# Graph attention: the bound and the multiply of three of 25 source blocks move from VectorE to GpSimd

## The reference, cut to what matters

```python
h = (x @ W).reshape(n, HEADS, C)
a_s = jnp.einsum('nhc,hc->nh', h, att_src)
a_d = jnp.einsum('nhc,hc->nh', h, att_dst)
e = jax.nn.leaky_relu(a_s[src] + a_d[dst], 0.2)
m = jax.ops.segment_max(e, dst, num_segments=n)
p = jnp.exp(e - m[dst])
z = jax.ops.segment_sum(p, dst, num_segments=n)
alpha = p / (z[dst] + 1e-16)
out = jax.ops.segment_sum(h[src] * alpha[:, :, None], dst, num_segments=n)
```

## Time and profile before

| what | value |
|---|---|
| median of three runs | 2292.35 us (2290.55 to 2293.96) |
| the profiled execution, its own time | 2294.51 us |
| its span | 2292.8 us |
| busy: TensorE, VectorE, ScalarE, GpSimd | 81%, 77%, 52%, 5% |
| mean granted TensorE clock | 0.94 |
| HBM traffic | 149 GB/s over the span |

### The profile page before, as it was taken

One profiled execution on the slowest core, in us unless ns is written; L12 is line 12 of the kernel. 1 busy time (PEld: TensorE's weight loads), 2 busy tenths in 40 slices (PEclk: granted clock), 3 DMA queues, 4 the chain that ended last, 5 costly groups with the idle time before them and its releaser, 6 DMA issues. The chain is left out here.

```text
span 2292.8 us, 43438 instructions
## 1 busy us (share of the span) xinstructions
PE 1856.6 (81%) x16035; PEld 1418.4 (62%) x16036; DVE 1761.2 (77%) x1796; ACT 1188.8 (52%) x2187; POOL 122.4 (5%) x224
## 2 busy tenths in 40 slices
PE   3566666699778988889888898884999999798793
PEld 2466666344566766667666676673888887455452
DVE  4999998000589999999999999956888887671474
ACT  1466666000577777777777777655666665101001
POOL 4000000100000000000000000000000000110120
PEclk9899999799999999999999999967999999899896
DMA  3598999999043134441344413343555550790691
GB/s 110 152 251 250 250 251 250 240 272 272 15 117 103 39 94 116 117 106 35 93 116 117 108 35 91 90 105 68 115 125 127 120 115 1 328 408 18 270 417 56
DMA packets 482537, 341.78 MB, mean 149 GB/s; under 512 B 322664, under 2 KB 474496, under 8 KB 475824
## 3 DMA queue, kind: packets, MB, share of 16 engines
q1 hardware_dynamic: 478096, 337.57, 52.6%
q10 hardware_dynamic: 3664, 1.68, 0.3%
q0 software_dynamic: 720, 1.77, 0.3%
HBM read 214.05 MB, written 126.94 MB: 149 GB/s over the span
## 5 line engine op out<-in xcount | busy, mean ns | idle before, releaser
L1195 ACT ACTIVATE exponentials<-gr_ps,att_cols 128x256 f32<-128x256 f32 (+1 forms) x1300 | 487.6, 486 | 183.2 <-PE gr_ps L1050 180.6
L1050 PE MATMUL gr_ps<-ident,gr_r 128*128 128x128 f32 (+1 forms) x2500 | 379.1, 291 | 69.1 <-DVE gr_r L1402 67.2
L1050 PEld LDWEIGHTS gr_ps<-ident,gr_r 128*128 128x128 f32 (+1 forms) x2500 | 284.5, 148 | 150.7 <-issue 126.1
L1083 PE MATMUL gr_ps<-exponentials,heads 128*33 128x128 f32 (+1 forms) x5000 | 358.0, 277 | 14.1 <-DVE exponentials L1408 14.1
L1408 DVE SCALAR_TENSOR_TENSOR exponentials<-exponentials,gr_count_t 128x3072 f32<-128x3072 f32 (+1 forms) x104 | 341.2, 3281 | 25.4 <-ACT exponentials L1195 24.6
L1369 DVE CUSTOM_DVE_ANT_0 gr_unread<-gr_src_rows,gr_closed 128x3125 bf16<-128x3125 f32 (+1 forms) x100 | 344.3, 3443 | 12.8 <-ACT gr_src_rows L1249 12.5
L519 PE MATMUL bm_ps<-bm_hot 128*100 128x100 bf16 (+1 forms) x3168 | 222.6, 226 | 120.3 <-DVE bm_hot L477 119.2
L1083 PEld LDWEIGHTS gr_ps<-exponentials,heads 128*33 128x33 f32 x5000 | 250.6, 112 | 78.2 <-issue 51.1
L519 PEld LDWEIGHTS bm_ps<-bm_hot 128*100 128x100 bf16 x3168 | 206.1, 126 | 136.9 <-DVE bm_hot L477 136.9
L553 ACT ACTIVATE bm_stage<-bm_ps 96x800 f32<-96x800 f32 x264 | 206.0, 829 | 137.9 <-PE bm_ps L519 136.7
L759 PE MATMUL sage_ps<-sage_counts,sage_parts 128*128 128x400 bf16 x1200 | 207.2, 337 | 14.9 <-DVE sage_counts L793 14.9
(11 more groups left out here) (304 smaller groups left out, 1894.2 us busy)
## 6 DMA issues: line engine op xcount, KB each, us to landing
sage_ring<-count_by_source SPq DMA_DIRECT2D x50, 1600.0 KB, 9.8
adjacency<-bm_stage SPq DMA_DIRECT2D x264, 300.0 KB, 3.2
count_pair<-adjacency SPq DMA_DIRECT2D x37, 1600.0 KB, 8.8
count_by_source<-gr_count_t SPq DMA_DIRECT2D x12, 3200.0 KB, 17.2
gr_src_rows<-adjacency SPq DMA_DIRECT2D x20, 1600.0 KB, 15.0
ar_counts<-adjacency SPq DMA_DIRECT2D x13, 1600.0 KB, 8.4
gr_count_t<-adjacency SPq DMA_DIRECT2D x5, 1600.0 KB, 14.8
count_by_source<-gr_count_t SPq DMA_DIRECT2D x1, 1600.0 KB, 11.8
```

Of the source, the lines that this page charges most:

```text
L1050: last = pe.transpose(ps[:, i % RINGS, c:c + n], r[0:n, slot(g, h) + j, s * P:(s + 1) * P], k.ident[0:n, 0:n])
L1083: last = pe.matmul(ps[j * PAIR:j * PAIR + C + 1, 7, 0:rows(g)], heads[:, h, s, :], e[:, s, c:c + rows(g)], start=s == 0, stop=s == NT - 1, ...
L1195: last = act.activation(e[:, s, places(g, h)], ps[:, i % RINGS, c:c + w], ACT.Exp, bias=cols[:, h, s:s + 1])
```

## The change

Blocks 22 to 24 of each head are no longer part of VectorE's second weighing, except in the last super tile. GpSimd does them in two instructions, a minimum with 1 and, after a wait for its own first one, a product with the counts. It waits for the same two semaphores as VectorE's second weighing. Its adds for super tile g+1 (`super_tile`) now stand between the parts of head 0 and of head 1 of super tile g. TensorE waits for the new semaphore `pooled` before chunk 11 (blocks 22 and 23), and ScalarE before it overwrites the later parts of `count_t`.

```diff
+        BY_POOL = 22
...
+        pooled, bounded, held_pool = sem("gr_pooled"), sem("gr_bounded"), sem("gr_held_pool")
...
+            def weigh_last(g, h):
+                hold(pool, raised, (g * HEADS + h) * PIECES + PIECES, held_pool)
+                if h == 0:
+                    hold(pool, taken_n, counts_done(g), held_pool)
+                part = e[:, BY_POOL:NT, :]
+                pool.tensor_scalar(part, part, 1.0, None, ALU.min).then_inc(bounded, 1)
+                pool.wait_ge(bounded, g * HEADS + (h + 1))
+                pool.tensor_tensor(part, part, count_t[:, BY_POOL:NT, :], ALU.mult).then_inc(pooled, 1)
+
+            def work(g, g_next):
+                weigh_last(g, 0)
+                super_tile(g_next)
+                for h in range(1, HEADS):
+                    weigh_last(g, h)
+
             super_tile(0)
...
-            with pool.Fori(1, LAST - 1) as g:
-                super_tile(g)
-            super_tile(LAST - 1)
-            super_tile(LAST)
+            work(0, 1)
+            with pool.Fori(1, LAST - 2) as g:
+                work(g, g + 1)
+            work(LAST - 2, LAST - 1)
+            work(LAST - 1, LAST)
...
             def gather_chunk(g, h, i):
                 if i == RINGS:
                     pe.wait_ge(weighed, (g * HEADS + h) * 2 + 2)
+                if i * BLOCKS == BY_POOL and not is_super(g, LAST):
+                    pe.wait_ge(pooled, g * HEADS + (h + 1))
...
                 else:
                     need(act, weighed, g * (2 * HEADS))
+                    need(act, pooled, g * HEADS)
...
-                weigh(g, h, CUT, NT)
+                weigh(g, h, CUT, NT if is_super(g, LAST) else BY_POOL)
```

## The result

| | before | changed |
|---|---|---|
| median of four runs each | 2291.45 us | 2383.48 us (2382.0 to 2384.89) |
| ratio, 95% interval | 1 | 1.040 (1.0382 to 1.0418) |
| span of the profiled execution | 2292.8 us | 2382.1 us |
| granted clock, mean | 0.944 | 0.927 |

The change costs 92 us. The forecast was 2357 (2318 to 2408), slower with 0.92. The direction was right and so was the main mechanism, VectorE held up by GpSimd. The size of +65 was 27 us short, and 12 of these come from a wait that the prediction had put at nothing.

A forecast was written before the change was run, and what follows sets the result against it. The prediction took an unbroken chain of VectorE instructions in the attention stage to bound the kernel. Added GpSimd delays less saved weighing gave +65 us on 2294.5; less 2.2 for the median, 2357 us (2318 to 2408).

The forecast's parts named there:

- The size of +65: Whole kernel: +1.49 us a head, 5.5 us a super tile, twelve 66 us, about 1 hidden in the last.
- What bounds the kernel: Attention stage: a chain of VectorE instructions without holes, busy 70.32 of 71.59 us a super tile.
- They take turns at boundaries: VectorE and GpSimd alternate at instruction boundaries; per head the product delays VectorE 1.62 us, the minimum 0.66.
- The sum of delays: Per head VectorE pays 0.66 + 1.62 us; three of eight delays a super tile are 0.14 us shorter.
- The saved 38 us: VectorE's second weighing loses 768 elements a partition, worth 0.79 us a head, -38 us over 48 heads.
- Where the two fall: Minimum after the head's last exponential, product one boundary later: each head pays two delays, +1.49 us net.
- What is late next: TensorE's gap before the turning in heads 2, 3 and 0 grows from 1.07 to about 3.1 us; costed at nothing.
- Rival C: TensorE falls behind: lowered clock in two more heads a super tile, first weighing too early; 40 us more, 2397, chance 0.1.
- my signs of being wrong: Other VectorE instructions keep 1.91 and 3.40 us, TensorE waits for GpSimd at L1083, or VectorE for ScalarE before a weighing.
- The new waits at nothing: TensorE's wait for `pooled` before chunk 11 is met 4 us early in head 0; ScalarE's long done; no cost.
- my case's own range: The +65 us case, its terms uncertain by a third: 2335 to 2385, chance 0.62.

The follow-up runs named there:

- e1: The changed kernel without GpSimd's two instructions: blocks 22 to 24 neither bounded nor multiplied, GpSimd only raises the semaphore; 2259.0 us, ratio 0.985.
- e2: The changed kernel without GpSimd's minimum, so blocks 22 to 24 are multiplied but not bounded; 2335.1 us, ratio 1.018.
- e9: The changed kernel with ten matmuls of zeros before TensorE waits for the rows of heads 0, 2 and 3, first 12 super tiles; 2365.8 us, ratio 1.0321.

## Why the prediction came out right in kind and short in size

- *What bounds the kernel.* Right. e1 takes 38 us off VectorE's instructions and 34 us off the time, and e2 adds 76 us with the product.
- *They take turns at boundaries.* Right for the product: forecast at 1.62 us, measured at 1.59 to 1.61, and at 1.48 inside a pair of rows. For the minimum the number was right, 0.66 us before a two-input instruction against 0.64, and the way to it was luck: I had taken 0.84 us for the whole instruction and 0.18 of it as hidden, while it ran for 1.99 us and held VectorE up for the first third. The sum of delays was forecast as 4 x 2.28 - 0.42 = 8.7 us a super tile, 105 in twelve, and is 110. The saved 38 us were right. The Trainium skill (SBUF — State Buffer, section "SBUF: two separate sides") gives the exclusion as a lock for the whole instruction; the minimum of 768 elements held `best` up for 0.64 us while its own row ran on to 1.99 us behind the start it was granted (1049.76 to 1051.75), so here the measurement differs from the page. At 1280 elements, 2.80 of 3.31 us, it comes near it.
- *Where the two fall.* Partly wrong. I had one delay from the minimum. Before a pair of row instructions it makes two of 0.49 us, and the product then falls behind the pair, before the weighing, at 1.61 instead of 1.48. In head 3 it costs `level` 0.39 us, less than I said. Dear and cheap ones nearly cancel, so that only 5 to 6 us are missing in the sum.
- *What is late next.* This is the step that failed: "I count nothing for it". The longer gaps were forecast rightly, 3.1 us against 3.12 before head 0, and the fall of the clock behind such a gap was named. I took the gap after which the clock falls from head 2, saw that VectorE had no wait behind it there, and carried this over to head 0. But head 0 has another chain behind its turns: the counts are turned and copied after the last exponential, and the second weighing waits for them. In the kernel before, the weighing starts at 938.78 and the copy ends at 938.25: 0.5 us of room, against a loss of 1.7 us in the turns. Rival C named the lowered clock but placed the wait at the first weighing, with 40 us. It was the count wait, 12 us, and e9, in which head 0's turns stay fast, gets 20 us back. One of my signs of being wrong came with it: "if VectorE waits for ScalarE before a weighing (C)".
- *The new waits at nothing.* Right for three blocks: the changed kernel's TensorE shows no wait for GpSimd. With five blocks it does, 27.6 us.
- *The range.* 2383 lies in my case's own range of 2335 to 2385, at its upper edge. That range was made for terms uncertain by a third; it also took in a wait that was not among them.

The remaining 6 us of VectorE's idle time in the changed kernel (9.3 against 6.6 us before the rows, 8.2 against 5.2 before the first weighing) were not taken apart.

## What to carry to other kernels

If VectorE sets the pace with instructions like those of this stage, which read two SBUF tensors or are as fast as the row instructions (1.91 us for 3125 elements), an element moved to GpSimd is not work taken off it: VectorE stood still for 2.1 ns per element of a product where its own pass cost 1.03 ns. Look for the evidence in the trace before: an existing small GpSimd instruction that takes three times its undisturbed time, and the VectorE instruction behind it that is longer by 0.13 or 0.27 us. And when a change makes one engine wait longer, ask for every chain that hangs on that engine's clock, not only for the one where a long gap is already seen, how much room its last waiter has.

## What the runs showed that I had not expected

- A minimum of 768 elements on GpSimd delays a two-input VectorE instruction by 0.64 us and each of two row instructions by 0.49 us; of 1280 elements it delays `best` by 2.80 us. The minimum itself runs in proportion to its length behind the boundary: 1.35, 1.99 and 3.31 us for 512, 768 and 1280 elements. What it holds up does not: 0.42, 0.64 and 2.80 us. The step in between was not searched.
- A MEMSET of 512 elements on GpSimd runs beside a two-input VectorE instruction at no cost to either (0.52 us, 3.41 us).
- A minimum on GpSimd that started 0.14 us before VectorE's next instruction was passed over twice and lasted 8.27 us.
- Ten matmuls of zeros, 1.80 us in a pause of over 3 us, made the changed kernel 20 us faster. In the kernel before they moved the fall of the clock from head 2 to head 3 and made it no faster.
